# Four seams of a four-layer graph kernel: a score row spread by TensorE, a projection in three rounded passes, decoder weights loaded a stage ahead, encoder features in pieces

## The reference

```
# layer 0: 8 heads of 64
feats = x @ kernels[h]; a_s = feats @ attn_self[h]; a_n = feats @ attn_neigh[h]
dense = exp(-(a_s[:, None] - a_n[None, :])**2) * (adj > 0)
out_h = (dense / (dense.sum(1) + EPS)) @ feats + biases[h];  relu(concat)
# layer 1
adj @ (x @ W) + b
# layer 2
e = leaky(s1[:, None] + s2[None, :] + a_b, 0.2), masked by adj > 0
softmax(e, 1) @ (x @ fc_w + fc_b)
# layer 3: 4 heads of 128, encoder and decoder
Xw = x_h @ W[h];  scores = sigmoid(f1[:, None] + f2[None, :]) weighted by the pattern
att = masked softmax(scores)           # the decoder uses the same weights again
enc = batchnorm(att @ Xw); mlp_block(enc); dec = att @ (enc @ W); mlp_block(dec)
```

## Time and profile before

| | us |
|---|---|
| median of 3 runs | 3274.81 |
| lowest, highest | 3272.9, 3275.7 |
| the profiled execution's own time | 3278.24 |
| its span (first to last instruction) | 3276.4 |
| TensorE busy, share of the span | 3023.8, 92% |
| VectorE busy, share | 2629.0, 80% |
| ScalarE busy, share | 1991.2, 61% |
| GpSimd busy, share | 293.1, 9% |

### The profile page before, as it was taken

One profiled execution on the slowest core, in us unless ns is written; L12 is line 12 of the kernel. 1 busy time (PEld: TensorE's weight loads), 2 busy tenths in 40 slices (PEclk: granted clock), 3 DMA queues, 4 the chain that ended last, 5 costly groups with the idle time before them and its releaser, 6 DMA issues. The chain is left out here.

```text
span 3276.4 us, 39399 instructions
## 1 busy us (share of the span) xinstructions
PE 3023.8 (92%) x15078; PEld 2182.7 (67%) x15078; DVE 2629.0 (80%) x3413; ACT 1991.2 (61%) x1863; POOL 293.1 (9%) x442
## 2 busy tenths in 40 slices
PE   6799999999978999995999986999999978899995
PEld 5533333333334888884788875888888845899995
DVE  5799999999967677675777746888888847798997
ACT  1499999999942212123444427888888804666665
POOL 0010101000002111110010010010000100000003
PEclk9899999999989999998999997999999989999997
DMA  6310110000014677777233318676676740899995
GB/s 249 126 67 26 67 42 17 17 9 17 9 61 147 233 287 269 272 259 288 106 125 121 110 66 315 238 276 253 259 271 243 270 153 33 313 317 311 315 312 180
DMA packets 158266, 577.11 MB, mean 176 GB/s; under 512 B 17467, under 2 KB 31507, under 8 KB 142976
## 3 DMA queue, kind: packets, MB, share of 16 engines
q1 hardware_dynamic: 132416, 432.86, 36.4%
q0 software_dynamic: 22784, 136.49, 11.8%
q10 hardware_dynamic: 2880, 5.24, 0.5%
HBM read 370.82 MB, written 203.70 MB: 175 GB/s over the span
## 5 line engine op out<-in xcount | busy, mean ns | idle before, releaser
L567 PE MATMUL bank<-dist,hf 128*65 128x512 f32 x1500 | 577.9, 542 | 0.3 <-ACT dist L529 0.2
L1509 PE MATMUL bank<-pt,HA 128*128 128x256 f32 x1936 | 504.4, 380 | 0.0
L567 PEld LDWEIGHTS bank<-dist,hf 128*65 128x65 f32 x1500 | 205.7, 138 | 359.4 <-issue 330.1
L1436 DVE COPY pt<-bank 128x512 f32<-128x512 f32 (+1 forms) x440 | 264.9, 632 | 111.2 <-PE bank L1497 109.0
L1509 PEld LDWEIGHTS bank<-pt,HA 128*128 128x128 f32 x1936 | 328.4, 191 | 23.4
L1497 PE MATMUL bank<-idt,v 128*128 128x128 f32 x1936 | 303.9, 278 | 42.6 <-ACT v L1383 25.9
L1785 DVE TENSOR_TENSOR w<-w,whi 128x1024 fp32r<-128x1024 f32 (+1 forms) x264 | 296.8, 1132 | 48.8 <-ACT whi L1748 43.5
L529 ACT ACTIVATE dist<-dist 128x1408 f32<-128x1408 f32 (+1 forms) x250 | 323.4, 1321 | 3.6
L1748 ACT ACTIVATE whi<-w 128x1024 fp32r<-128x1024 f32 (+1 forms) x264 | 257.6, 986 | 111.5 <-DMA w<-weights 96.7
L1497 PEld LDWEIGHTS bank<-idt,v 128*128 128x128 f32 x1936 | 245.1, 143 | 107.4 <-ACT pt L1390 23.9
L1714 PE MATMUL bank<-whi,EH 128*128 128x256 f32 x968 | 283.0, 292 | 17.1 <-DVE w L1785 11.3
(11 more groups left out here) (206 smaller groups left out, 5957.9 us busy)
## 6 DMA issues: line engine op xcount, KB each, us to landing
weights<-pt SPq DMA_DIRECT2D x220, 512.0 KB, 3.7
w<-weights SPq DMA_DIRECT2D x176, 512.0 KB, 6.9
w<-weights SPq DMA_DIRECT2D x88, 384.0 KB, 5.0
at<-in_adj_tiles SPq DMA_DIRECT2D x22, 1408.0 KB, 8.3
rows<-in_adj_rows SPq DMA_DIRECT2D x22, 1408.0 KB, 6.9
HB<-in_adj_rows POOLq DMA_DIRECT2D x22, 1354.0 KB, 7.2
rows_low<-HB POOLq DMA_DIRECT2D x22, 1354.0 KB, 5.3
rows<-rows_low POOLq DMA_DIRECT2D x22, 1354.0 KB, 7.8
```

The source lines that it names most:

```text
L567: mm = pe.matmul(sums_bank(hh, k)[0:FW, 0:hi - a * P], hf[hh][:, m, :], d[:, a * P:hi], start=(m == 0), stop=(m == T - 1))
L1436: dve.tensor_copy(dst, src).then_inc(kept_dve, 1)
L1509: t = pe.matmul(acc_t[n % 2][:, 0:P2], HA[:, m, h * D3:(h + 1) * D3], pt[n % 2][:, m, :, :].rearrange("p r n -> p (r n)"), start=(m == 0), ...
```

## The change

1. *Head scores spread by TensorE.* In the projection of layer 0, after tile 13, TensorE transposes the first 11 score columns of head 0, each broadcast to 128 columns, and ScalarE copies the result into `first_scores`, which takes the place of the first score buffer. The first head's load is left out. `hf` and GpSimd's copies go, and TensorE reads the columns of `HA`.
2. *Second projection in three rounded passes.* The projection of layer 1 gets the scheme of layer 0. ScalarE rounds the weights, VectorE writes their low part and that of each turned tile. GpSimd takes over the bias addition. SP loads the weights behind the first two tiles of x.
3. *Decoder weights a stage ahead.* The first three pieces are loaded in the MLP stage, and the first two are split there, ScalarE in chunk 3 and VectorE in chunk 4.
4. *Encoder features in pieces.* SP first waits for the two adjacency rows, then issues the features in three pieces with the rows of heads 2 and 3 between them. Head 1's row is made by 22 transposes of broadcast columns and six copies on VectorE. A few semaphores are shared for this.

The diff, cut to its core:

```diff
# 1
+                            if j == CT + 2:
+                                pe.wait_ge(proj_out, CT)
+                                for t in range(CT):
+                                    mm = pe.transpose(turn[t // 4][:, t % 4 * P:(t % 4 + 1) * P],
+                                                      scol[:, 0, t:t + 1].broadcast_to([128, P]), idt[:, :])
+                                mm.then_inc(head_turned, 1)
...
+                            if 2 * i + q == CT + 3:
+                                act.wait_ge(head_turned, 1)
+                                for k, (a, b) in enumerate(((0, 4), (4, 8), (8, CT))):
+                                    act.activation(first_scores[:, a * P:b * P], turn[k][:, 0:(b - a) * P], ACT.Copy)
...
-            sB = [sb(ph, f"sB{q}", [P, CW]) for q in (0, 1)]
+            sB = [first_scores, sb(ph, "sB1", [P, CW])]
...
+                                if group(c, hp, hh) > 0:
+                                    sp.dma_start(sB[hh][:, 0:VALID[c]],
...
-                                pool.tensor_copy(hf[hh][:, :, :], HA[0:P, :, bass.ds((hp * 2 + hh) * FW, FW)])\
-                                    .then_inc(hf_ready, 1)
...
-                                        mm = pe.matmul(sums_bank(hh, k)[0:FW, 0:hi - a * P], hf[hh][:, m, :],
+                                        mm = pe.matmul(sums_bank(hh, k)[0:FW, 0:hi - a * P], HA[0:P, m, (hp * 2 + hh) * FW:(hp * 2 + hh + 1) * FW],
# 2
+                    sp.dma_start(bias[:, :], b0.partition_broadcast(P)).then_inc(w_in, 16)
+                    for j in range(T):
+                        wait(sp, r_full, j - 1)
+                        sp.dma_start(xin[j % 2][:, :], x[j]).then_inc(x_in[j % 2], 16)
+                        if j == 1:
+                            sp.dma_start(w_sb[:, :, :], w1).then_inc(c_in, 16)
...
+                    def turned_low(j):
+                        dve.wait_ge(turned_out, T + j + 1)
+                        wait(dve, proj_mm, T + j - 1)
+                        dve.tensor_tensor(xtl[j % 2][:, :, :], etp_view(), xth[j % 2][:, :, :].bitcast(FP32), ALU.subtract)\
+                           .then_inc(low_out, 1)
...
-                        dve.tensor_tensor(R[q][:, :], HB[0:P, j, :], bias[:, :], ALU.add).then_inc(r_half, 1)
...
                         ln_moments(dve, j, q, R, st)
+                        if j == 1:
+                            dve.wait_ge(split_w, 1)
+                            dve.tensor_tensor(wl[:, :, :], w_sb[:, :, :], wh[:, :, :].bitcast(FP32), ALU.subtract).then_inc(split_w, 1)
+                        if j >= 1:
+                            turned_low(j - 1)
                         if j >= 3:
                             h_out(j - 3)
...
+                    for j in range(T):
+                        ln_power(pool, j, j % 2, st)
+                        pool.wait_ge(ln_done, j + 1)
+                        if j + 2 < T:
+                            biased(j + 2)
+                        pool.dma_start(xs[0][j], xn[j % 2][:, :]).then_inc(xn_stored[j % 2], 16)
...
+                            pe.matmul(into[j % 2][0:P, :], xth[j % 2][:, k, :], wh[:, k, :], start=(k == 0), stop=False)
+                            pe.matmul(into[j % 2][0:P, :], xth[j % 2][:, k, :], wl[:, k, :], start=False, stop=False)
+                            t = pe.matmul(into[j % 2][0:P, :], xtl[j % 2][:, k, :], wh[:, k, :], start=False, stop=(k == KT - 1))
# 3
+                    for k in range(AHEAD):
+                        sp.dma_start(w_ahead[k][:, :, :].bitcast(FP32), weights[0][:, 4 * k:4 * k + 4, :]).then_inc(ahead_in[k], 16)
...
+                            if c == 3 and f < SPLIT_AHEAD:
+                                act.wait_ge(ahead_in[f], 16)
+                                act.activation(whi_ahead[f][:, :, :], w_ahead[f][:, :, :].bitcast(FP32), ACT.Copy)\
+                                   .then_inc(whi_ready, 1)
...
+                            if k >= AHEAD:
+                                sp.dma_start(w[k % WS][:, 0:b - a, :].bitcast(FP32), weights[n][:, a:b, :]).then_inc(w_in[k % WS], 16)
# 4
+            HA_PARTS = [(0, 8), (8, 15), (15, T)]
...
+                    for r in (0, 1):
+                        sp.wait_ge(rows_in[r], 16)
+                    for k, (a, b) in enumerate(HA_PARTS):
+                        sp.dma_start(HA[:, a:b, :], xw_dram[a:b].rearrange("t p d -> p t d")).then_inc(*ha_part[k][0])
+                        if k + 2 < H3:
+                            sp.dma_start(fB[k + 2], rows3[k + 2, 0:N].partition_broadcast(P)).then_inc(fb_in[k + 1], 16)
...
+                    for g, (a, b) in enumerate(GROUPS):
+                        width = min(b * P, N) - a * P
+                        dve.wait_ge(rows_turned, 2 + 2 * NG + 1 + g + 1)
+                        dve.tensor_copy(fB[1][:, a * P:a * P + width], spread[g][:, 0:width]).then_inc(fb_in[0], 1)
...
+                    for g in range(NG):
+                        spread_scores(pe, g, lambda t: f3[:, 1, 1, t:t + 1], 4 * T)
```

More of the change, by code:

```diff
@@ L650, in _ @@
                         ln_write(dve, j, q, R, st, xn[q][:, :])
-                    for j in range(T - 3, T):
+                    h_out(T - 3)
+                    turned_low(T - 1)
+                    for j in (T - 2, T - 1):
                         h_out(j)
@@ L922, in multiplied @@
                 return MULS.index((j, g)) + 1 if (j, g) in MULS else NG * j + g + 1
-            v_in = [sem(f"v_in{k}") for k in range(len(V_PARTS))]
+            v_in, V_ALL = [sem(f"v_in{k}") for k in range(len(V_PARTS))], 32
             t_hi = sem("l2_t_hi")
@@ L1503, in mul @@
                         for m in range(lo, hi):
+                            if n == 0:
+                                for k, part in enumerate(HA_PARTS):
+                                    if m == part[0]:
+                                        pe.wait_ge(*ha_part[k][1])
                             if m == 0 and n >= 2:
@@ L1763, in second @@
                            .then_inc(e_ready, 1)
-                    for k in range(HS - 1):
+                    for k in range(SPLIT_AHEAD, HS - 1):
                         split(k)
```

87 lines of the change are left out of this document (39 added, 48 removed).

## The result

The changed kernel takes **3253.43 us** (median of 4 runs, 3252.15 to 3256.35) beside 3275.26 (4 runs, 3272.9 to 3278.5) for the kernel before on the same chip: ratio 0.9927, interval 0.9915 to 0.9939, so 23.9 us less by the ratio and 21.8 by the medians. The forecast was 3254.7. The profiled execution took 3252.15 (span 3250.3), 26.1 us less span than the profiled execution of before.

The account below looks back on a forecast made before the run. TensorE's own work bounds the long stages, so only seams between stages can gain: -3.9 - 5.8 - 4.9 - 5.5 = -20.1 us off the median 3274.8 gives 3254.7. Own bounds 3246 to 3262; range with rivals 1 to 3, 3245 to 3267.

Parts of the forecast that it names:

- A: First attention: start 4.4 us earlier, transposes in the projection before cost 1.2, copies removed give 0.7; sum -3.9 us.
- the bound of 0: Projection of layer 0: lower bound for the transposes' price, if hidden behind VectorE's long fold; 1.2 us was taken.
- The copies: First attention: removing GpSimd's copies of head features frees 16 us of VectorE, counted as 0.7 us (bounds 0 and 3).
- B: Projection of layer 1: start 1.5 us later, tiles save 4.0, end saves 3.3; sum -5.8 us (bounds -8 and -2).
- The steady part: Projection of layer 1: twenty tiles at 3.70 us instead of 3.90, GpSimd and VectorE almost tied; saves 4.0 us.
- C: Decoder's start: the matrix lands earlier, 10.0 us in, with three pieces loaded ahead; -4.9 us (bounds -1.3 and -6.1).
- D: Encoder attention's start: TensorE restarts about 33 us in, not 39, as rows land first; -5.5 us (bounds -7.5 and 0).
- 1 (the encoder's loads only change places): Encoder attention: bandwidth is the limit and head 3's row lands when it did; gain 1 us, time 3259; chance 0.12.
- 2 (the matrix needs its 11.5 us): Decoder's start: the matrix takes 11.5 us however little lies ahead; gain 1.3 us, time 3258; chance 0.08.
- 3: Projection of layer 1: GpSimd bounds it mildly, 3.9 to 4.3 us per tile; -2 to +6, time 3259 to 3267; chance 0.10.
- 4: Projection of layer 1: GpSimd's additions held up to 3.4 us, tile 5.8; +36 us, time 3297; chance 0.04.
- 5 (eaten within the stages): All seams: earlier starts eaten by TensorE's slow clock after gaps or the decoder's DMAs; time 3268 to 3275; chance 0.06.

Follow-up runs that it names:

- D alone: Kernel before with only the encoder features in pieces behind the two rows and head 1's row by TensorE: ratio 0.9976, stage 691.82 us (before 697.48).
- B alone: Kernel before with only layer 1's projection in three rounded passes and its bias addition on GpSimd: ratio 0.9957, stage 95.23 us (before 104.46).
- A alone: Kernel before with only head 0's scores spread by TensorE and GpSimd's feature copies removed: ratio 0.9989, stage 821.90 us (before 826.49).

## Why the prediction was right, point by point

- **What bounds the kernel: right.** Only the seams moved; the untouched stages moved by no more than they scatter, and the seams' differences sum to the kernel's.
- **A: -4.6 in the two profiles, -5.2 in the means; forecast -3.9.** The start was right to 0.1 (4.37 and 4.46 earlier, forecast 4.4). The transposes did not cost 1.2. The step that failed is "with TensorE never idle, so the transposes are on the path": it was read from tiles later on the earlier trace rows, while the tile that they were put in has 3.01 us of idle time behind it. The text named the bound of 0 for this very reason, and took 1.2; the other side, that work in the gap would spare the next tile its slow clock, is in none of its bounds, and brought about 0.9. The copies: forecast 0.7; what is left of the stage's difference beside the start is 0.2 to 0.9, and 1.7 without anything else. The size is near, and the reason is half right: "TensorE has no gap there" rests on a window that begins at 550, and in the first half it was VectorE that set the pace. The near size is in part luck, as 6.8 us of lead were won and 5.0 lost again.
- **B: -8.6 in the two profiles, -8.7 in the means; forecast -5.8, bounds -8 and -2.** The result lies outside these bounds. Start +1.7 (forecast +1.5) and end -3.2 (-3.3) were right. The steady part is -7.1, not -4.0: the mis-sized term is the tile, 3.47 and not 3.70 (that would make 4.6 over 20 tiles; the one tile of 4.96 gives 1.5 of it back). That GpSimd and VectorE are tied was right, and both were put 0.1 to 0.2 too long. GpSimd's addition is done 2.24 us after the write's start (0.62, then 1.68 of which 0.06 overlap with the next), not 0.54 + 0.6 + 1.25 = 2.39: of the two-input instruction's length it waits about 1.68 - 1.25 = 0.43, not all 0.6, as it comes to it 0.16 after its start. The store and the power take 1.18 and not 1.25. VectorE's own tile is 3.47 and not 3.6. Small errors, but times 20. (TensorE's 12 x 0.23 + 0.43 is 3.19 and not 3.17, which changes nothing.) That the addition waits for that one instruction was argued from the earlier trace rows, and is now shown by 1.67 against 1.30, and by the pair at 951.32. The Trainium skill's rule in "SBUF — State Buffer", "Who interferes with whom", lets the first to issue win, and the traces agree, in both orders: with VectorE 0.16 ahead its instruction stays 0.68 and the addition takes 1.68, with GpSimd 0.06 ahead the addition stays 1.25 and VectorE's takes 1.74.
- **C: restart 4.3 earlier in the two profiles and 4.0 in the means, stage -5.7 and -3.8; forecast -4.9.** The second piece came 10.4 to 11.0 us in (mean 10.6, forecast 10.0), from 14.6 in the mean. Of the miss of 0.9, 0.6 is the model of rate and latency, and 0.3 that a single profile's 14.87 was taken as the kernel's.
- **D: restart -5.5 in the two profiles, -4.9 in the means, stage -5.7 and -5.0; forecast -5.5.** The steps came within 1 us of where they were put: VectorE had the two rows 6.4 and 9.6 us in (forecast 6.6 and 10.2), the second exponential started at 15.6 (16.4), and head 3's row, the last to be late, was there at 30.6 (29.6).
- **The sum.** -20.1 against -22.8 in the means: B was 2.9 and A 1.3 short, C 1.1 and D 0.5 too large. The mechanism was right at each seam; that the time came within 1.3 us of the forecast is partly luck, since these errors cancel in part and the total is only known to about 4 us.

The rivals: 1 (the encoder's loads only change places) is out, D alone made the stage 5.7 us shorter. 2 (the matrix needs its 11.5 us) is out, it took 8.8 from issue to TensorE's restart. 3 and 4 (GpSimd bounds B, mildly or badly) did not come about, but 4's arithmetic holds: at 4.69 per tile the whole gain is gone. It was 1.2 us of GpSimd per tile away. 5 (eaten within the stages) is out by the tables of stages.

What stays open: the ratio of B alone (14.1 us, 4 on either side) is larger than its stage's gain (9.2). Its profiled execution had a shorter decoder (446.0), but that is one of the stages that scatter without the change, and no row shows a cause.

The scatter of the other stages is explained only in part. In the projection of layer 0 it goes with the clock behind TensorE's gaps, as above. In the first attention the seven profiles with A fall into two groups: three of 820.4, in which the granted clock of the first 20 us was 0.81, and four of 821.6 to 821.9, in which it was 0.73 to 0.75. In the attention of layer 1 the longest (454.2, with A alone) has ten waits of TensorE of over 0.5 us for VectorE's results where after has four. What made VectorE late there is not known.

## What to carry to other kernels

Where the long stages are saturated, read the instants between them: for each seam find the one load that lands last, and count only by how much that instant moves. Ask of each wait where its data is first needed: in the decoder, one wait moved by five heads was worth about 5 us (444.1 in the mean against 438.65 and 439.87), more than the three loads moved ahead of it (3.8). Count a gap of TensorE with the slow matmuls behind it: 1.4 us of other work in a gap of 3 us made the next tile 1.3 to 2.7 us shorter here. And when work goes to an idle engine, work out how long its whole chain per tile is, with what it must wait for, since it may be tied already; the idle share of the span (GpSimd 91%) doesn't tell it.

## What the runs showed of the hardware that was not expected

- The same GpSimd addition of 512 columns took 1.25 us with nothing of VectorE beside it and 1.67 when a two-input VectorE instruction had started 0.16 us earlier. In the other order, with the addition 0.06 us ahead, it kept its 1.25 and VectorE's instruction took 1.74 instead of 0.68.
- TensorE's clock behind a gap. In the projection of layer 0 a gap of 3.01 us was followed by a tile at a granted clock of 0.51 to 0.70 in all five profiles without the transposes (an equal gap two tiles earlier spared the next tile in four of twelve); with eleven transposes in it and 1.81 us of idling left, the clock stayed at 1.00 in all seven. In the decoder's start matmuls ran at the lower level for 4.6 us behind a gap of 8.90, and for 2.8 us behind one of 3.14.
- A row of TensorE that is busy throughout does not say that TensorE sets the pace: with 52.88 us busy of 53.02 a head still became 1.1 us shorter when VectorE's waits for GpSimd's copies went.
